# Networks 2 and 3: VectorE's 52 steps of a pass in straight code instead of a loop, and last steps without preparation

## The reference, cut to what matters

```python
# network 2, four layers, 8 heads of 16
alpha = sum(q[dst] * k[src], axis=-1) / 4
a = softmax of alpha over the edges of one dst
out = segment_sum(a * v[src], dst)
# network 3, once, 4 heads; q, k and v each get a term from the edge's attributes
compat = einsum('ehd,ehd->eh', q[s] * scale + edge_attr @ q_rpe_w + q_rpe_b, k[t] + ...)
attn = softmax of compat over the edges of one s
out = segment_sum((v[t] + ...) * attn, s)
```

## Time and profile before

| | us |
|---|---|
| median of 3 runs | 12631.28 (12626.98 to 12631.36) |
| the profiled execution's own time | 12619.18 |
| its span in the profile | 12617.4 |
| PE busy | 7549.2 (60%) |
| DVE busy | 7916.2 (63%) |
| ACT busy | 6282.0 (50%) |
| POOL busy | 8891.0 (70%) |

### The profile page before, as it was taken

One profiled execution on the slowest core, in us unless ns is written; L12 is line 12 of the kernel. 1 busy time (PEld: TensorE's weight loads), 2 busy tenths in 40 slices (PEclk: granted clock), 3 DMA queues, 4 the chain that ended last, 5 costly groups with the idle time before them and its releaser, 6 DMA issues. The chain is left out here.

```text
span 12617.4 us, 185971 instructions
## 1 busy us (share of the span) xinstructions
PE 7549.2 (60%) x46394; PEld 5746.9 (46%) x46395; DVE 7916.2 (63%) x21707; ACT 6282.0 (50%) x14083; POOL 8891.0 (70%) x9142
## 2 busy tenths in 40 slices
PE   6666455555551112343666676667666766667998
PEld 5666322232220002333466546663666366645766
DVE  8888666666662224333677767776777677775555
ACT  8333233333333333665566546664666366635666
POOL 0777677767767775777777677776777677766775
PEclk9766677767765555565777787778777877775555
DMA  0000111121121113223444544454444444432223
GB/s 33 2 2 2 31 39 39 39 38 39 39 38 39 40 40 48 54 53 52 132 132 132 118 111 133 131 125 105 132 133 132 96 133 131 133 74 58 72 71 63
DMA packets 820582, 949.30 MB, mean 75 GB/s; under 512 B 481147, under 2 KB 557360, under 8 KB 820156
## 3 DMA queue, kind: packets, MB, share of 16 engines
q0 software_dynamic: 343040, 637.31, 22.0%
q1 hardware_dynamic: 477244, 309.04, 9.2%
HBM read 859.26 MB, written 86.39 MB: 75 GB/s over the span
## 5 line engine op out<-in xcount | busy, mean ns | idle before, releaser
L808 POOL DMA_INDIRECT work<-t,idx x3328 | 3176.7, 955 | 1107.3 <-issue 1014.2
L1658 POOL DMA_INDIRECT work<-t,idx x3328 | 3177.6, 955 | 1024.0 <-issue 1013.4
L820 ACT ACTIVATE work<-iota,loc 128x128 f32<-128x128 f32 (+1 forms) x6672 | 2034.6, 387 | 3253.0 <-DVEq L1110 1921.9
L1113 DVE TENSOR_TENSOR work<-work,ps 128x192 f32 x2496 | 882.8, 354 | 1233.2 <-PE ps L1137 933.6
L1137 PE MATMUL ps<-work 128*128 128x192 bf16 x2496 | 412.7, 305 | 1764.1 <-SPq L815 1702.5
L1753 PE MATMUL ps<-work 128*128 x6784 | 1334.1, 379 | 140.9 <-ACT work L833 81.9
L1753 PEld LDWEIGHTS ps<-work 128*128 128x128 f32 x6784 | 1315.6, 297 | 179.5 <-issue 165.4
L1765 PE MATMUL ps<-work 128*128 128x136 f32 x6656 | 1264.8, 348 | 10.9 <-DVE work L1819 10.1
L600 POOL DMA_INDIRECT tab<-work x784 | 863.1, 1101 | 562.0 <-DVE work L453 315.0
L1137 PEld LDWEIGHTS ps<-work 128*128 128x128 bf16 x2496 | 232.4, 113 | 2077.8 <-issue 1069.8
L728 POOL DMA_INDIRECT tab<-work x784 | 818.7, 1044 | 462.7 <-issue 248.2
(11 more groups left out here) (426 smaller groups left out, 17006.6 us busy)
## 6 DMA issues: line engine op xcount, KB each, us to landing
work<-t,idx POOLq DMA_INDIRECT x7488
node<-pl SPq DMA_DIRECT2D x424, 256.0 KB, 3.4
work<-pl SPq DMA_DIRECT2D x54, 512.0 KB
work<-pl SPq DMA_DIRECT2D x106, 256.0 KB, 3.3
tab<-work POOLq DMA_INDIRECT x1568, 2.1
t<-work SPq DMA_DIRECT2D x196, 128.0 KB, 1.8
x<-work SPq DMA_DIRECT2D x196, 64.0 KB, 1.7
h<-work SPq DMA_DIRECT2D x28, 448.0 KB, 2.6
```

The source lines that it names most:

```text
L808: pool.indirect_dma_start(X[:, j % 4, n, :], None, table, bass.IndirectOffsetOnAxis(ap=idx[k][:, 8 * j + n:8 * j + n + 1], axis=0)).then_i ...
L820: t = act.activation(P[:, b, n, :], iota[:, :], ACT.Square, scale=-1.0, bias=loc[k][:, bass.ds(a + n, 1)])
L1113: added.on(dve.tensor_tensor(av, av, part(z, n), ALU.add))
L1658: pool.indirect_dma_start(X[:, j % 4, n, M - KD:W], None, table, bass.IndirectOffsetOnAxis(ap=idx[k][:, NT * j + n:NT * j + n + 1], axis=0 ...
```

## The change

On VectorE the loop of both passes becomes a loop of the generator: `for i in range(1, Q // 4 - 1)`, so every step has its own instructions, at addresses that are constants. The seams with their semaphore instructions stay. The last four steps are written apart on all engines. PE and ACT keep a loop of 11 turns and have the last four steps in straight code behind it.

In these last steps the preparation is left out. In step 51 PE makes no queries, ACT no node one-hots, VectorE no scores: a new function `adds` does the four additions that stood between the score instructions. In network 3 the argument `ahead` also takes the attribute splits, squares and one-hots out of steps 50 and 51. SP no longer loads places or attributes beyond step 51. Waits for what is no longer made are gone too.

```diff
 # attend (network 2)
 def act_step(act, a, w, first, last=False):
...
-                    onehot_nodes(act, own, PT, LB, lb, lbfree, 0, ptd)
+                    if not last:
+                        onehot_nodes(act, own, PT, LB, lb, lbfree, 0, ptd)
...
 def pe_step(pe, a, w, first, last=False):
...
-                    queries(pe, a + NT, 0)
+                    if not last:
+                        queries(pe, a + NT, 0)
...
-                    pe.wait_ge(usedp.sem, usedp.up())
-                    queries(pe, a + NT, 1)
+                    if not last:
+                        pe.wait_ge(usedp.sem, usedp.up())
+                        queries(pe, a + NT, 1)
...
-                    with pe.Fori(1, Q // 4) as i:
+                    with pe.Fori(1, Q // 4 - 1) as i:
                         for w in range(4):
                             pe_step(pe, i * (4 * NT) + NT * w, w, False)
                         for s in waited:
                             s.back(pe)
+                    for w in range(4):
+                        pe_step(pe, NT * (Q - 4 + w), w, False, w == 3)
+                    for s in waited:
+                        s.back(pe)
...
+                def adds(dve, u, i):
+                    av = places(dve, u, i)
+                    dve.wait_ge(parts.sem, parts.up())
+                    for n in range(4 * i, 4 * i + 4):
+                        add(dve, av, n)
...
-                    scores(dve, (w + 1) % 4, 1 - u, 0, 1, has1)
+                    if final:
+                        adds(dve, 1 - u, 1)
+                    else:
+                        scores(dve, (w + 1) % 4, 1 - u, 0, 1, has1)
...
-                    scores(dve, (w + 1) % 4, 1 - u, 1, 2, has1)
+                    if final:
+                        adds(dve, 1 - u, 2)
+                    else:
+                        scores(dve, (w + 1) % 4, 1 - u, 1, 2, has1)
...
-                    with dve.Fori(1, Q // 4) as i:
+                    for i in range(1, Q // 4 - 1):
                         for w in range(4):
                             dve_step(dve, i * (4 * NT) + NT * w, w, False)
                         dve.wait_ge(v.sem, v.c)
                         for s in waited:
                             s.back(dve)
+                    for w in range(4):
+                        dve_step(dve, NT * (Q - 4 + w), w, False, w == 3)
+                    dve.wait_ge(v.sem, v.c)
+                    for s in waited:
+                        s.back(dve)
 # network3
-                def dve_step(dve, a, w, first):
+                def dve_step(dve, a, w, first, ahead=2):
...
-                    split_rest(dve, u)
+                    if ahead == 2:
+                        split_rest(dve, u)
...
-                    with dve.Fori(1, Q // 4) as i:
+                    for i in range(1, Q // 4 - 1):
...
+                    for w in range(4):
+                        dve_step(dve, NT * (Q - 4 + w), w, False, min(3 - w, 2))
```

More of the change, by code:

```diff
@@ L1708, in exponentials, with act_step @@
                                    ACT.Exp).then_inc(ex.sem, 1)
-                def act_step(act, a, w, first):
+                def act_step(act, a, w, first, last=False):
                     u = w % 2
@@ L1766, in weigh_, with pe_step @@
                     t.then_inc(parts.sem, 1)
-                def pe_step(pe, a, w, first):
+                def pe_step(pe, a, w, first, last=False):
                     u, b1 = w % 2, (w + 3) % 4
@@ L2778, in _ @@
                             s.back(act)
+                    for w in range(4):
+                        act_step(act, NT * (Q - 4 + w), w, False, min(3 - w, 2))
+                    for s in waited:
+                        s.back(act)
                     act.wait_ge(pfree.sem, pfree.up(2))
@@ L2819, in weigh_, with pe_step @@
                     t.then_inc(parts.sem, 1)
-                def pe_step(pe, a, w, first):
+                def pe_step(pe, a, w, first, last=False):
                     u, b1 = w % 2, (w + 3) % 4
                     has1 = not (first and w == 0)
-                    turned(pe, 1 - u, 0)
+                    if not last:
+                        turned(pe, 1 - u, 0)
                     pe.wait_ge(evd.sem, evd.up())
@@ L2833, in pe_step @@
                         weigh_(pe, b1, 1 - u, 1)
-                    views(pe, a + NT, 1 - u, 0)
+                    if not last:
+                        views(pe, a + NT, 1 - u, 0)
                     pe.wait_ge(rowd.sem, rowd.up())
@@ L2839, in pe_step @@
                         weigh_(pe, b1, 1 - u, 2)
-                    turned(pe, 1 - u, 1)
+                    if not last:
+                        turned(pe, 1 - u, 1)
                     pe.wait_ge(md.sem, md.up())
@@ L2844, in pe_step @@
                         weigh_(pe, b1, 1 - u, 3)
-                    pe.wait_ge(used.sem, used.up())
-                    views(pe, a + NT, 1 - u, 1)
+                    if not last:
+                        pe.wait_ge(used.sem, used.up())
+                        views(pe, a + NT, 1 - u, 1)
                 @block.tensor
@@ L2866, in _ @@
                             s.back(pe)
+                    for w in range(4):
+                        pe_step(pe, NT * (Q - 4 + w), w, False, w == 3)
+                    for s in waited:
+                        s.back(pe)
                     for i in range(4):
                         weigh_(pe, 3, 1, i)
-                    pe.wait_ge(evd.sem, evd.up())
-                    pe.wait_ge(onehot.sem, onehot.up())
-                    pe.wait_ge(split.sem, split.up())
-                    pe.wait_ge(weight.sem, weight.up(2))
                     for s in waited:
```

79 lines of the change are left out of this document (47 added, 32 removed).

## The result

| | kernel before | changed kernel |
|---|---|---|
| median | 12631.32 us (12626.98 to 12641.88, 6 runs) | 12580.28 us (12568.25 to 12582.21, 6 runs) |
| ratio, 95% interval | | 0.9957, 0.9944 to 0.9969 |
| span of the profiled execution | 12617.4 us | 12580.4 us |

What follows compares the result with a forecast made beforehand. Network 3 was taken as bound by PE, with idle time at VectorE's seams, network 2 by POOL and, at pass ends, landing gathers. 33.1 + 9.0 + 23.4 = 65.5 us takes 12631.3 to about 12566 us; range 12546 to 12601.

Steps and rivals of the forecast that it cites:

- Network 3's seams: VectorE's 11 taken-branch seams in network 3 fall from 4.06 to 1.05 us each in straight code: 33.1 us gained.
- Network 3's end: Shortened last steps of network 3, preparation left out: 9.0 us gained, bounds 7 and 10.
- Network 2's ends: Shortened last steps in network 2's four passes: 6.1 us in the first, 23.4 us in all, bounds 18 and 26.
- Rival 3: Instruction fetches meet the crowded end of network 2's passes: 10 us a pass, 40 us of gain lost, 12606; chance 0.07.
- Rival 2: Network 3's straight code waits for the same fetch, or PE's seam takes its place: 33 us lost, 12599; chance 0.12.
- rival 4: VectorE waits for fetches in straight code, 144 us in network 2, some 30 us of it slack: slower, 12713; chance 0.06.
- POOL is the bound: In network 2 only POOL's own issue, 0.3 us each, stands before a gather; VectorE follows some microseconds behind.
- The seams of network 2: Unrolling VectorE in network 2 saves branch and register instructions, hardly more than 3.0 us a turn; counted as nothing.

Runs made afterwards that it cites:

- e1: Kernel before with only network 3's VectorE loop written out, no ends shortened: 32.5 us faster than the kernel before, ratio 0.9975.
- e5: Kernel before with the first instruction of network 3's VectorE loop laid on slot 0 of a fetch block: 27.7 us faster, ratio 0.9978.
- e6: Kernel before with the first instruction of network 3's VectorE loop laid on slot 100: 0.1 us faster, ratio 1.0.
- e9: The changed kernel run once more, on another chip: 58.8 us faster than the kernel before, ratio 0.9953.
- e10: Changed kernel, but SP issues network 2's next flags between its waits for the two halves of a step's gathers: 66.2 us faster than before, ratio 0.9949.
- e12: Changed kernel with network 2's VectorE loops kept on slot 0 and SP's flags in network 2 issued earlier: 65.6 us faster than before, ratio 0.9951.
- e2: Kernel before with only network 2's VectorE loops written out, all ends as before: 20.0 us faster than the kernel before, ratio 0.9982.
- e11: Changed kernel, but network 2's four VectorE loops kept, 11 turns each, on slot 0: 64.7 us faster than the kernel before, ratio 0.9952.
- e7: Kernel before with network 2's four VectorE loops on slots 100, 228, 78 and 196, network 3's on 100: 70.5 us slower, ratio 1.0056.
- e3: Changed kernel with VectorE's straight code made loops again in both networks, only the ends shortened: 19.9 us slower than the kernel before, ratio 1.0016.
- e4: Changed kernel, except that network 2's VectorE keeps a loop of 11 turns: 9.4 us faster than the kernel before, ratio 0.9992.
- e8: Shortened ends in both networks, VectorE loops of 11 turns kept, all five laid on slot 0: 54.6 us faster than the kernel before, ratio 0.9958.

## Why the prediction was right, step by step

**Network 3's seams: right in size, by a reason that was half right.** 33.1 us were forecast. The stretch from scan to scan shows 1075.7 - 1043.3 = 32.4, and in e1, where nothing else changed, 1075.7 - 1044.7 = 31.0, with medians 32.5 apart. PE's 0.69 us of idle time and steps of 20.2 us came as written. That the cost is of the taken branch and of the loop's place is shown by e5 and e6, which have the same body on two slots; that it is the wait for a fetch follows from the packets, 6 against 50, which come and go with it. What fell is the sentence behind it, that network 3's body is fetched anew and network 2's isn't, as if it were a matter of the bodies. Both bodies can be cheap, and both can be dear. Of the 33 us, 28 could be had by laying the loop on another slot.

**Network 3's end: right.** 9.0 us forecast, 16.1 - 7.3 = 8.8 measured.

**Network 2's ends: each right, their sum not all kept.** 6.1 us forecast for the first pass, and 34.35 - 28.2 = 6.15 in the trace; 23.4 for four, and 22.6 in the trace from step 51's scans on. As a share of the whole, the term of 23.4 us was the one mis-sized: with network 3's 41.3 us taken off, 10 us are left of the first measurement's 51 and 17.5 of e9's 58.8. In e10 to e12, without late flags or without straight code in network 2, the gain is 64.7 to 66.2 us. That this is the 65.5 of the sum is in part luck: e10's tails are 7.3 us a pass shorter than those of before, 44.9 against 52.2 on average, where 5.9 were forecast, and other stretches take some of it back. I had written that VectorE waits for data whose time POOL and the DMA engines set, and that 52 us would become 46. The first trace has 48.2 to 50.5. The wait for flags did grow as written, from 2.2 to 7.5 us before to 9.6 to 11.8 (some 8 were forecast for the first pass); what I left out is that the flags themselves could come later. What the first profile lacks beside that, 12.8 us of longer gather stretches, isn't tied to any edit.

**Rival 3 was in part what happened.** I had priced flags that meet the crowded end of a pass at 10 us a pass, 40 us in all. In the first trace late flags cost some 2.5 us a pass, in e9 0.9 us. That VectorE's own fetches are what delays them isn't shown: e2 has the same straight code, and its scan of step 50 comes 2.7, 2.1 and 2.6 us ahead of the last gather's start in three passes and 1.1 behind in one, much as in kernels that loop (e5: 2.9 and 2.8 ahead, 0.4 and 0.7 behind). What made all four passes of the first trace late is open. Two pairs of kernels (e2 and e1, e9 and e11), in network 2's stretch and in the medians, put straight code in network 2 some 6 to 9 us behind the loop, each less than its uncertainty; a third, e10 and e12, has it 4.2 us ahead in the stretch and level in the medians.

**Rival 2 and rival 4 were wrong**, for the reason given against them: straight code has its fetches ahead of time. But a step of rival 4's arithmetic fell too. I allowed network 2 some 30 us of slack against stalls of VectorE. In e7 and e3 there is none: stalls of 49.9 - 11 x 1.6 = 32 us made e7's first pass 35 us longer, since VectorE's lag, from a step's last gather to its first scan, ran up to 22 to 24 us and POOL then waited for its buffers. VectorE has no speed to spare there, which "POOL is the bound" hid: in the trace of before this lag already grows from 7 us at the start of the first pass to 16 us at its end.

**The seams of network 2 at nothing: true here, and luck.** I valued the unrolling of network 2 at zero. Against the kernel before it is. But with the shortened ends in and the loops kept, the code moves and two of the four loops become dear. Then e3 is 20 us slower than before, where my terms for the ends (23.4 + 9.0) said 32 faster. Against such a kernel unrolling network 2 is worth some 42 to 49 us (e4's -9.4 against the changed kernel's -51.0 and -58.8, neither taken beside e4). A sum of terms that are each right can miss by 50 us if an edit moves code ahead of a loop.

## What to carry to other kernels

Before crediting a loop or its removal, look at the idle time behind each taken branch, pass by pass. Where one body shows two prices, the price is the place of the code, so it can be had by placing the loop and it can be lost by any edit ahead of it. A wait that hides a gain (here the flags) has to be followed to the next wait under it, which here was the landing of the last gathers with PE's queries close behind. And a stretch that no edit touched, here the gathers of a pass, has to be compared on one chip before its change is put down to the edit.

## What the runs showed of the hardware

- The branch back of one and the same loop body of VectorE costs 1.3 to 1.6 us a seam or 3.95 to 5.2 us, by where the body stands. The slots tried fit blocks of 128 instructions, of which a body may touch three: 303 instructions from slot 78 (to 380) and from 68 cheap, from 100 dear; 338 from 0 cheap, from 100 dear. A limit on the head's slot alone, between 78 and 100, fits them too.
- With straight code on VectorE there are 31 instruction packets of 8 KB in 735 us, some 25 of them VectorE's by the estimate above, and no wait for issue over 0.3 us.
- A second instruction queue of the profile, q8, has packets of 16 KB (75, 1.23 MB in the changed kernel, and as many in e3, where VectorE loops), so a block's size isn't the same for all engines.
- The jump to a loop that was laid on a slot is a wait of 4.2 to 4.5 us, the seam's 1.6 us in it, once in each of e7's two cheap passes. It isn't always one: e5's and three of e8's five ways in took 1.6 to 1.9 us, e8's other two 4.2 and 5.4.
